# VectorE's order at the end of a step: the low half of the second norm ahead of the second residual

## What is computed

```python
x = x + _L0_conv_ref(_gn(x), weight, bias)          # depthwise 31x31 convolution of the group norm
x = x + _L1_conv_ref(_gn(x), ln1, wq.., wo, ln2, w1, b1, w2, b2)
# _L1: roll by (-3,-3), cut into 7x7 windows, and for the 49 tokens t of each window:
t = t + softmax(q k^T / sqrt(8)) v @ wo + bo        # q, k, v from _ln(t), 12 heads of 8
t = t + gelu(_ln(t) @ w1 + b1) @ w2 + b2            # 96 -> 384 -> 96
# and roll back
```

## Time and profile before

| | us |
|---|---|
| median of 3 runs | 5445.11 |
| lowest and highest | 5443.77, 5454.63 |
| the profiled execution | 5449.83 |
| its span, first to last instruction | 5448.0 |
| mean granted TensorE clock | 0.982 |

### The profile page before, as it was taken

The page is one execution under the profiler, slowest core; times in us unless marked ns, Lnnn a source line. Parts: engine busy times, 40 slices in busy tenths (PEclk is TensorE's granted clock), DMA queues, the critical chain, the costliest instruction groups (busy, mean ns, idle before and its releaser), DMA issues.

```text
span 5448.0 us, 229437 instructions
## 1 busy us (share of the span) xinstructions
PE 5203.4 (96%) x97360; PEld 4039.8 (74%) x97360; DVE 3400.9 (62%) x5852; ACT 3474.8 (64%) x5334; POOL 3510.0 (64%) x4814
## 2 busy tenths in 40 slices
PE   5999999999779999999999999999999999999998
PEld 5999999999746666666666666666666666666665
DVE  2333333433347767777777777777777777777775
ACT  2444444444357767777777777777777777777776
POOL 2222222222258878888888888888888888888886
PEclk9999999999859999999999999999999999999999
DMA  4444444444256666666666666666666666766663
GB/s 124 119 127 118 120 123 118 119 122 125 57 114 148 148 136 147 145 146 146 147 149 145 148 148 146 151 147 144 149 147 147 148 147 147 148 149 149 149 150 81
DMA packets 1099821, 740.56 MB, mean 136 GB/s; under 512 B 465428, under 2 KB 1070708, under 8 KB 1098708
## 3 DMA queue, kind: packets, MB, share of 16 engines
q1 hardware_dynamic: 1069620, 687.18, 56.0%
q0 software_dynamic: 29184, 38.71, 3.4%
HBM read 409.02 MB, written 316.46 MB: 133 GB/s over the span
## 4 chain that ended last, share of the span: by engine, by line
PE 44%; DMA 10%; SPq 8%; POOL 3%; issue 3%; DVE 2%; ACT 2%; DVEq 0%; ACTq 0%; POOLq 0%
PE ps_ring L1697 12%; DMA b_q_st<-row_maxima 10%; PE ps_pv L1769 7%; PE ps_ring L1780 5%; SPq L1347 4%; PE ps_s L1723 3%; PE ps_t L1723 3%; PE ps_ring L1706 3%; PE ps_xc L1838 2%; POOL b_outs L1448 2%; PE ps_ring L1708 2%; PE ps_ring L1707 2%; SPq L1339 2%; SPq L1333 1%; PE ps_ring L1812 1%
## 5 line engine op out<-in xcount | busy, mean ns | idle before, releaser
L225 POOL TENSOR_SCALAR xn<-xin,aff 96x896 f32<-96x896 f32 x192 | 174.0, 906 | 1070.3 <-DVE aff L375 1057.6
L1586 DVE TENSOR_REDUCE b_mx<-ps_s 113x12 f32<-113x588 f32 x1024 | 781.1, 763 | 113.2 <-PE ps_s L1723 113.1
L1393 POOL TENSOR_TENSOR b_mid_lo<-b_mid,b_mid_hi 128x392 fp32r<-128x392 f32 x768 | 788.3, 1026 | 43.3
L1769 PEld LDWEIGHTS ps_pv<-b_vd,b_probs_t 128*49 128x49 f32 x24576 | 612.2, 127 | 161.0 <-issue 151.9
L1487 ACT ACTIVATE b_probs_t<-ps_t 128x588 f32<-128x588 f32 x1024 | 664.6, 649 | 103.2 <-PE ps_t L1723 101.8
L410 PE MATMUL ps_conv<-blocks_hi,toep_hi 128*128 128x288 f32 (+2 forms) x2880 | 666.6, 313 | 0.0
L1769 PE MATMUL ps_pv<-b_vd,b_probs_t 128*49 128x18 f32 x24576 | 663.0, 200 | 0.2 <-issue 0.2
L410 PE MATMUL ps_conv<-blocks_hi,toep_lo 128*128 128x288 f32 (+2 forms) x2880 | 653.6, 308 | 0.0
L410 PE MATMUL ps_conv<-blocks_lo,toep_hi 128*128 128x288 f32 (+2 forms) x2880 | 653.1, 308 | 0.0
L1448 POOL TENSOR_TENSOR b_outs<-b_y,b_xs 96x392 f32<-96x392 f32 x256 | 317.3, 1240 | 494.7 <-DVE b_y L1669 494.7
L282 ACT ACTIVATE toep_hi<-toep 128x640 fp32r<-128x640 f32 x288 | 197.1, 748 | 632.8 <-PE ps_conv L410 616.7
(11 more groups left out here) (147 smaller groups left out, 12062.2 us busy)
## 6 DMA issues: line engine op xcount, KB each, us to landing
stacked_qk<-b_planes SPq DMA_DIRECT2D x512, 220.5 KB, 3.1
b_q_st<-stacked_qk SPq DMA_DIRECT2D x512, 220.5 KB, 4.4
b_k_st<-stacked_qk SPq DMA_DIRECT2D x512, 220.5 KB, 5.6
toep<-filters_padded SPq DMA_DIRECT2D x96, 936.5 KB, 13.8
stacked_qk<-b_planes SPq DMA_DIRECT2D x512, 147.0 KB, 2.7
stacked_qk<-b_planes SPq DMA_DIRECT2D x512, 73.5 KB, 2.1
b_xs<-x_scratch SPq DMA_DIRECT2D x224, 147.0 KB, 2.8
out<-b_outs SPq DMA_DIRECT2D x224, 147.0 KB, 3.3
```

Source lines behind the costliest of these rows:

```text
L1393: pool.tensor_tensor(mid_lo[:, m, :], mid[:, m, :], mid_hi[:, m, :].bitcast(F32), ALU.subtract).then_inc(S["mid_split"], 1)
L1586: dve.tensor_reduce(mx[0:rows_q, :].rearrange("q (e m p) -> q e m p", e=2, p=PAIRS)[:, :, :, p], ps_s[0:rows_q, :, 0:HPAIR * TOK].rearrang ...
L1769: ins = pe.matmul(to, pt[:, p, at:at + TOK], vd[:, m % VR, p, h, :, :], start=True, stop=True, skip_group_check=True)
```

## The change

DVE's `h2_lo` moves ahead of `y`; both keep their waits and their semaphores:

```diff
                     dve.tensor_tensor(h2[:, :], xc2[:, :], rstd[:, :], ALU.mult).then_inc(S["h2_done"], 1)
+                if proj is not None:
+                    dve.wait_ge(S["h2_high"], proj + 1)
+                    dve.wait_ge(S["h2_done"], proj + 1)
+                    dve.tensor_tensor(h2_lo[:, :], h2[:, :], h2_hi[:, :].bitcast(F32), ALU.subtract).then_inc(
+                        S["h2_split"], 1)
                 if mlps is not None:
                     dve.wait_ge(S["w2_ps"], mlps + 1)
                     after(dve, i, "added", mlps - 1)
                     dve.scalar_tensor_tensor(y[:, mlps % 2, :], bank(i, s, "w2")[0:C, 0:NT], cols[0:C, B2:B2 + 1],
                                              t1[:, mlps % 2, :], ALU.add, ALU.add).then_inc(S["y_done"], 1)
-                if proj is not None:
-                    dve.wait_ge(S["h2_high"], proj + 1)
-                    dve.wait_ge(S["h2_done"], proj + 1)
-                    dve.tensor_tensor(h2_lo[:, :], h2[:, :], h2_hi[:, :].bitcast(F32), ALU.subtract).then_inc(
-                        S["h2_split"], 1)
             steps(dve, step)
```

More of the change, by code:

```diff
@@ L1023, in step @@
                                              t1[:, mlps % 2, :], ALU.add, ALU.add).then_inc(S["y_done"], 1)
[L1024 to L1110, removed]
```

496 lines of the change are left out of this document (removed).

## The result

The change made the kernel slower: 5491.03 us at the median of 12 runs (5457.68 to 5521.38), against 5446.86 us for the kernel before in 12 runs. The ratio is 1.0082, 95% interval 1.0056 to 1.0108. In the changed kernel `y` is L1027, `h2_lo` L1022, `outs` L801, the last piece of the maxima L814, the score products L1076; in the kernels of the experiments these numbers differ by a few lines.

The account below looks back on a forecast made before the run. PE and the chain feeding the row-maxima read were taken as bounds together. Later reads of 41 - 13 = 28 us, times 0.46, gave +13 us: 5458 us from a 5445.1 median, range 5443 to 5490.

Parts of the forecast that it names:

- the bound and the mechanism: Window pass: PE and the chain feeding the row-maxima read bound together; a later last maxima piece delays the read one for one.
- `outs` shorter by 0.27 us: POOL's `outs`: with `h2_lo` done before it starts, it falls from 1,241 ns to near 970 ns.
- The working with `h2_hi`: `h2_hi` beside POOL's L1439: 922 ns median, 561 least, 0.50 us overlap; both pairs lose 0.12 to 0.14 us less than they overlap.
- R1: Rival on `outs`: relief equals the whole 0.39 us overlap, so no change, 5445 us; chance 0.16.
- R2: Rival on `outs`: no relief, it stays at 1,241 ns; +45 us, 5490 us; chance 0.18.
- I take 0.50: DVE: where `y` finds its product ready, it starts 0.50 us later, from 0.47 plus up to 0.1 for a semaphore instruction.
- the row maximum after the pair starts when it did: DVE: the row maximum following `h2_lo` and `y` keeps its start time, no delay.
- the share of 0.46: PE at `ps_t`: it pays for 0.46 of the reads' added lateness, taken between 0.34 and 0.60.
- stops of about 78 us: PE at `ps_t`: stops at the row maxima rise from 64.5 us to about 78, in more than 87 stops.
- 28 x 0.46 = 13 us: Sum for the window pass: 28 us of later reads (41 less 13) times PE's share gives 13 us slower.
- R3: Rival: steps where `y` waits for PE become the rule, chain gains 0.17 us each; -20 us, 5425 us; chance 0.07.
- R4: Rival: the 0.23 us delay is swallowed downstream in SP's issues or the read's landing; 5445 us; chance 0.07.

Follow-up runs that it names:

- e1: Kernel before, with POOL making the last maxima pieces ahead of `outs` and SP storing after the maxima reads; DVE order unchanged: ratio 0.9891.
- e2: Same POOL and SP edits as e1, but with the change's DVE order (`h2_lo` ahead of `y`): ratio 0.9896 to the kernel before.
- d2: Kernel before, DVE untouched, with a 0.73 us memset on POOL between its wait for `y` and `outs`: ratio 1.0123.
- d4: The change plus a second copy of the `h2_lo` subtraction (two SBUF inputs) on DVE behind `y`: ratio 1.0206 to the kernel before.
- d5: The change plus a 542 ns memset, reading no SBUF, on DVE behind `y`: ratio 1.0100 to the kernel before.
- e3: Kernel before with `y` one place further forward on DVE, between `h2_hi` and `h2`: ratio 1.0784.
- g1: f1_pool_only plus six 0.73 us memsets ahead of the maxima on POOL in 16 of 256 steps: ratio 1.0082 to the kernel before.
- c0_before: Control: the kernel before without its uncalled function: ratio 0.9998 to the kernel before.
- f1_pool_only: Kernel before with only POOL's order changed, the last maxima pieces ahead of `outs`; SP's store stays in place: ratio 0.984. Also written f1.
- f1_again: The same kernel as f1_pool_only, run again on the chip of g1: ratio 0.9864 to the kernel before.
- f2: Kernel before with only SP's part changed, the store issued after the reads of the maxima; POOL as before: ratio 0.9922.
- d1: Kernel before, DVE untouched, with a 0.36 us memset on POOL between its wait for `y` and `outs`: ratio 1.0005.

## Why the prediction was wrong

**Right: the bound and the mechanism.** The time went where the chain of waits said, `y`, `outs`, the maxima, SP's queue, the read, PE at `ps_t`. e1 and e2 show that without this chain the swap is free, d2 that a delay on it alone gives the loss. The sign was right. Nothing else took the place of the wait.

**Right: `outs` shorter by 0.27 us** (measured 0.256 in after, 0.255 between d4 and d5). The working with `h2_hi` in the prediction is borne out as well: there, in `h2_lo` beside `outs`, and in `e3` the other way round (0.73 us beside each other, 0.59 us longer) the loss is 0.13 to 0.14 us less than the overlap. R1, a relief of 0.39 us, would have shown `outs` at about 850 ns, and it never goes under 960 in any kernel. By the Trainium skill ("SBUF — State Buffer", "Who interferes with whom") the whole overlap would have come back; the measurement decides against it here, while the pairing of a two-input DVE instruction with a POOL instruction that reads SBUF is borne out by d4 and d5. R2, no relief, falls by the same rows, though its 5490 is nearest to the result.

**Wrong: "I take 0.50" for `y`.** It is 0.67 us in the step shown. I had bounded the extra semaphore instruction with up to 0.1 us and then taken nearly nothing of it, and I had given the pair `h2_lo`, `y` the overlap of 0.08 us that the pair `y`, `h2_lo` has before. After it there is a gap of 0.04 us. The row for that was there: `y` stood 0.04 us behind `h2` in the step of before, which it doesn't wait for. The maxima are then 0.67 - 0.256 = 0.41 us late, not 0.23. For the same reason "the row maximum after the pair starts when it did" is wrong: it starts 1.25 us after the end of `h2`, and 1.05 before (3005.85 and 3002.31). `e2` shows that this costs nothing.

**Wrong, the other way: the share of 0.46.** By my estimate, with 0.41 in 179 steps (73 us) and 0.15 - 0.26 = -0.11 in 76 (-8 us), the reads are some 65 us later; PE's stops grew by 15.6 us, 0.24 of it. Against the 56.2 us of `c0_before` the growth would be 23.9, and the share 0.37. The feedback that I had named, a stop giving the next read slack, may be stronger than I assumed; nothing here tests it. That I had forecast stops of about 78 us, and they are 80.1, is luck: two errors cancelled, within a scatter of 8 us. The 14.7 us that I gave for PE's own work in a step doesn't follow from its row (3,588.5 / 256 = 14.0); nothing rests on it.

**Wrong: a stop was priced at its own length.** This is the step that failed in the time. The sum has 28 x 0.46 = 13 us of stops and no term for the clock, but behind some of its stops PE also runs at the lower clock, and `g1` shows that a stop of 2 us then costs 8. What a us at the lower level costs comes from `g1`, 0.41 to 0.42, and from the runs: a line through time against time at the lower level has a slope of 0.40 over the 12 runs of the change, and of 0.39 over 29 runs of before (17 of them, and the 12 of `c0_before`).

The profiled pair alone doesn't show this share. PE's stops at the maxima over all steps, in the changed kernel and then in the one before, and the stretch at the lower clock between the two passes, first before and then after:

```profile
PE ps_t L1076 <- DMA b_q_st<-row_maxima: 84.3, 118, 2.3
...
PE ps_t L1723 <- DMA b_q_st<-row_maxima: 65.7, 90, 1.9
...
1467.30:1614.10 146.80, 81.56 (x1183) 50.30 (x1183) 50.35 (x100) 60.49 (x84) 70.26 (x80) 0.50 0.47 99
...
1467.90:1621.50 153.60, 89.00 (x1259) 55.19 (x1260) 53.94 (x108) 63.32 (x89) 72.75 (x82) 0.50 0.47 101
```

The stops grew by 18.6 us (15.6 from 1,740 us on), and 0.40 x (220 - 197) = 9 us of clock make up the rest of the 26.6 us and 1 more. But of the 23 us more at the lower clock only 10 stand behind stops at the maxima (48 us for 38), 7 in the stretch shown and 6 in the tail of the pass. The stretch shown begins 130 us before the first `h2_lo` (1,598 us), and time at the lower clock before 1,740 us is 133 us in `f1_pool_only` and 154 in `f1_again`, which are one kernel. So by this estimate some 4 us of clock in this pair go with the stops, and nothing ties the other 5 to the change.

The other runs have more of it. The mean clock of the 12 runs of the change is 0.978. That of before is 0.983 over the 29 runs named, 0.981 and 0.980 in two other sets of 17 and 0.981 in one of 11; the clock of the runs that the change was timed beside isn't on record. The difference, 0.0027 to 0.0049, x 2 x 5480 is 30 to 54 us, and at 0.40 some 12 to 22 us. With the stops that makes 28 to 40 of the 44 us between the medians, and 4 to 16 stay unassigned. `d5`, the nearest kernel to the change with before's clock on record beside it, is 55 us slower on the average: 29 by stops and, with 268 us at the lower clock for 209, 24 by the clock. The same sum fits `d2` (114 us longer in span: 52 of stops, 62 by the clock at 0.40) and falls 13 us short in `d4` (151: 65 and 73). In the runs of the change, the one at a clock of 0.987 took 5457.68 us, the one at 0.973 took 5521.38. The clock's share in before's own runs was on the page; I read it as a constant.

**R3, faster,** was right in one observation, fewer waits of `y` (28 for 77), but those steps never became the rule. **R4** falls with f2 and d2: half a us earlier or later at this place reaches PE.

## What to carry to other kernels

Where TensorE is nearly always busy, a stop can cost more than its length: look at the granted clock behind it as well as at the sum of the waits. A stop of 2 us cost four times its length here (`g1`), and in `e3` stops of 0.75 us in nearly every step cost about three times theirs. When a chain to a DMA read ends on the critical path, put the operations that feed it first on every engine that it passes, and leave work that TensorE doesn't wait for, here POOL's `outs`, behind them; this kernel gains 1.4 to 1.6% by that alone (f1), more than the order of the pair `h2_lo`, `y` gives or takes in the kernel as it stands. A VectorE instruction with two SBUF inputs lengthened the GpSimd one beside it, which reads SBUF, by less than they overlapped (0.26 us for 0.39), and a shift that merely moves the two apart already returned it (`d1`).

## What the runs showed of the hardware that I had not expected

A single stop of 1.97 to 2.03 us in the midst of a pass in which PE is busy 99% of the time (3555.64 of 3600.00 us in `f1_again`) was followed in 16 of 16 cases by 6.8 to 17.1 us at the 1.2 GHz level. In the change's own trace the stop ahead of the stretch shown is 1.63 us long. A long stop does not always do it: `d1` has ten stops of 1.36 us or more in its window pass, one of them 2.46 us at the maxima, and the clock falls behind a single one, of 1.50 us; of the ten longest stops in before five are followed by a fall, in the change's own trace four of ten. Nor does it take a long one, as `e3` shows with 34 falls and no stop above 0.9 us. What decides isn't settled. Such scatter in the clock would explain, though no run here tests it, why the runs of one kernel lie 30 to 60 us apart, and why `d1`, with more stops than before, is no slower. At the lower level this kernel loses 0.39 to 0.42 us for each us, and not half; in the stretch of the changed kernel shown above PE starts 15.4 matmuls per us, and 24.3 behind it, a loss of 0.37.

On DVE, `h2_lo`, which waits for two semaphores of DVE's own, the later one set by the instruction just before it, starts 0.11 us after that one's end (3004.60 to 3004.71, and 3008.62 to 3008.73 in `e3`); the instruction with the single wait in the earlier trace rows starts 0.04 us after.

And POOL's `outs` keeps a DVE instruction back as well as the other way round. In `e3` `h2` comes first, and `outs` is lengthened beside it to 1232 ns while `h2` stays at 552; then `h2_lo` starts beside `outs` and takes 1154 ns at the median instead of 563, and POOL's next piece of the maxima, beside its rest, 590 ns instead of 273. So a step pays in three places there for what cost it 0.26 us in one before.
